# A delta-rule block solve on TensorE taken in two halves of its twenty groups

## What is computed

```python
def delta_attn(x, Wq, Wk, Wv, Wb, Wo, onorm_w):      # b = 5, t = 64, H = 8, DK = DV = 32
    q = l2norm(jax.nn.silu((x @ Wq).reshape(b, t, H, DK)))
    k = l2norm(jax.nn.silu((x @ Wk).reshape(b, t, H, DK)))
    v = jax.nn.silu((x @ Wv).reshape(b, t, H, DV))
    beta = jax.nn.sigmoid(x @ Wb) * 2.0
    def step(S, inps):
        qi, ki, vi, bi = inps
        pred = jnp.einsum('bhkv,bhk->bhv', S, ki)
        S = S + bi[..., None, None] * ki[..., :, None] * (vi - pred)[..., None, :]
        o = jnp.einsum('bhkv,bhk->bhv', S, qi)
        return (S, o)
    _, o = jax.lax.scan(step, S0, (qt, kt, vt, bt))
    return rmsnorm(o, onorm_w).reshape(b, t, H * DV) @ Wo
for l in range(2):
    x = x + delta_attn(rmsnorm(x, norm1_w[l]), ...)
    g, y = jnp.split(rmsnorm(x, norm2_w[l]) @ Wg[l], 2, axis=-1)
    x = x + jax.nn.silu(g) * y @ Wd[l]
```

## Time and profile before

| | |
|---|---|
| median of 3 runs | 403.05 us (402.88 to 404.66) |
| time of the profiled execution | 402.49 us |
| its span, first to last instruction | 400.7 us |
| PE matmul busy | 310.2 us, 77% of the span, 4346 records |
| DVE busy | 201.9 us, 50% |
| ACT busy | 87.7 us, 22% |
| chain that ended last | PE 47%, DVE 31%, DMA 9%, ACT 5%, POOL 4%, issue 3% |
| mean granted PE clock | 0.872 of full speed |

### The profile page before, as it was taken

The page is one execution under the profiler, slowest core; times in us unless marked ns, Lnnn a source line. Parts: engine busy times, 40 slices in busy tenths (PEclk is TensorE's granted clock), DMA queues, the critical chain, the costliest instruction groups (busy, mean ns, idle before and its releaser), DMA issues.

```text
span 400.7 us, 9465 instructions
## 1 busy us (share of the span) xinstructions
PE 310.2 (77%) x4346; PEld 228.6 (57%) x4346; DVE 201.9 (50%) x349; ACT 87.7 (22%) x181; POOL 44.1 (11%) x33
## 2 busy tenths in 40 slices
PE   0999459968972597794776999895676999878965
PEld 0556355757862385472775767573676757555442
DVE  3029977994677443107553222107653232169992
ACT  1132012202210023452111133344121122231120
POOL 0744940200403000000000000000000000000000
PEclk9999958999995578899596799998695699989998
DMA  8999900000000000000000030410000000000001
GB/s 186 334 324 212 362 10 1 2 0 1 2 0 0 0 0 2 0 0 2 3 0 3 2 106 2 151 71 2 3 0 3 2 0 2 1 1 0 2 0 33
DMA packets 2521, 18.26 MB, mean 46 GB/s; under 512 B 441, under 2 KB 761, under 8 KB 1729
## 3 DMA queue, kind: packets, MB, share of 16 engines
q1 hardware_dynamic: 2497, 17.91, 14.6%
HBM read 17.58 MB, written 0.33 MB: 45 GB/s over the span
## 4 chain that ended last, share of the span: by engine, by line
PE 47%; DVE 31%; DMA 9%; ACT 5%; POOL 4%; issue 3%; SPq 1%; DVEq 0%; ACTq 0%; POOLq 0%
PE ps L1221 9%; DMA big<-in_patches 9%; PE ps L1066 5%; PE ps L1217 5%; PE ps L1006 4%; PE ps L1364 3%; POOL xs L262 3%; PE ps L1285 2%; PE ps L1327 2%; DVE big L888 2%; PE ps L1304 2%; PE ps L1016 2%; DVE big L916 2%; DVE qa L569 2%; DVE wt L913 2%
## 5 line engine op out<-in xcount | busy, mean ns | idle before, releaser
L1016 PE MATMUL ps<-big,cwb 120*128 120x384 f32 x120 | 43.6, 523 | 10.3 <-DMA big<-in_patches 10.3
L1016 PEld LDWEIGHTS ps<-big,cwb 120*128 120x128 f32 x120 | 24.4, 207 | 27.1 <-issue 14.3
L1217 PE MATMUL ps<-cst,ones 128*128 128x320 f32 x112 | 37.7, 488 | 0.0
L1066 PE MATMUL ps<-wkvg,pecT 128*128 128x256 f32 x144 | 32.0, 381 | 4.8 <-ACT big L360 4.8
L1221 PE MATMUL ps<-cwb,wl 128*128 128x320 f32 x120 | 33.2, 434 | 0.0
L1066 PEld LDWEIGHTS ps<-wkvg,pecT 128*128 128x128 f32 x144 | 27.0, 190 | 8.6 <-DVE prod L684 3.7
L1217 PEld LDWEIGHTS ps<-cst,ones 128*128 128x128 f32 x112 | 24.0, 219 | 10.6 <-issue 3.9
L1221 PEld LDWEIGHTS ps<-cwb,wl 128*128 128x128 f32 x120 | 22.6, 190 | 10.4 <-issue 0.9
L1285 PE MATMUL ps<-wt,big 32*32 32x32 f32 x1280 | 16.2, 209 | 13.2 <-DVE wt L891 10.5
L262 POOL TENSOR_TENSOR xs<-xs,big 120x640 f32<-120x640 f32 x14 | 23.0, 1645 | 8.2 <-DMA big<-in_patches 7.3
L1285 PEld LDWEIGHTS ps<-wt,big 32*32 32x32 f32 x1280 | 14.5, 121 | 15.3 <-DVE wt L891 11.4
(11 more groups left out here) (224 smaller groups left out, 483.8 us busy)
## 6 DMA issues: line engine op xcount, KB each, us to landing
big<-in_patches SPq DMA_DIRECT2D x6, 900.0 KB, 26.0
wl<-in_layers SPq DMA_DIRECT2D x2, 2176.0 KB, 27.0
wt<-in_tok SPq DMA_DIRECT2D x1, 2304.0 KB, 17.6
wf<-in_ffn SPq DMA_DIRECT2D x1, 2112.0 KB, 26.3
wl<-in_layers SPq DMA_DIRECT2D x2, 1040.0 KB, 23.2
cwb<-in_conv SPq DMA_DIRECT2D x1, 600.0 KB, 5.1
out<-h SPq DMA_DIRECT2D x5, 64.0 KB, 2.0
cst<-in_constants SPq DMA_DIRECT2D x1, 304.0 KB, 39.6
```

The costliest lines, as they stand in the source:

```text
L1016: last = mm(ps[:, i % 4, 0:GRP], cwc[:, k, c * P:(c + 1) * P], xg[:, g, k, :], start=(k == 0), stop=(k == KC - 1))
L1066: last = mm(ps[:, 2 * w + un % 2, t * C:(t + 1) * C], pecT[:, c, i * P:(i + 1) * P], wkvg[:, c, w * C:(w + 1) * C], start=(c == 0), stop=( ...
L1217: mm(ps[:, bank, 0:NT], ones[:, :], cst[:, 0:NT], start=True, stop=True)
```

## The change

All five steps, and the squares and their sums, go in halves `b` = 0 and 1 of ten groups, one bank each. The ACT and DVE instructions of 640 columns become two of 320, and every semaphore of the part is raised once (or, `b2`, twice) per half. PE starts the first half of the first solve when `t` is 1. The output product's first half waits besides until all additions to `bv` are done, since it overwrites the bank that they read. Matmuls, and the data they work on, stay as they are in number and size.

```diff
@@ -166,9 +166,9 @@
 
             return ps[r, b, 0:NT].rearrange("p (g n) -> p g n", n=32)
 
-        def both(x, q):
-
-            return x[32 * q:32 * q + 32, :, :].rearrange("p (a g) n -> p a (g n)", a=2)
+        def half(x, q, b):
+
+            return x[32 * q:32 * q + 32, NB * b:NB * (b + 1), :].rearrange("p g n -> p (g n)")
 
         ident = cst[:, K_ID:K_ID + P]
         blk = cst[:, K_BLK:K_BLK + P]
@@ -198,8 +198,8 @@
         EACH = {
             "lwa": 16, "lwb": 16, "x": 4, "n_sq": 2, "n_ms": 2, "n_rs": 4, "h": 4, "k_mm": 1, "q2_mm": 1, "bt_mm": 1,
             "v_mm": 1, "silu": 10, "ss_mm": 2, "rkq": 4, "kq": 5, "wbx": 1, "ap_mm": 3, "ap": 3, "y_mm": 2 * (LEVELS - 1), "pairs": 8, "y": 2 * (LEVELS - 1),
-            "z_mm": 2 * (LEVELS - 1), "tp": 2 * (LEVELS - 1), "t": 0, "u1_mm": 1, "u1": 1, "u1_two": 1, "r_mm": 1, "b2": 2, "u2_mm": 1, "u2": 1, "u2_two": 1,
-            "o_mm": 1, "osq": 1, "oss": 1, "ors": 2, "on": 1, "o_t": 1, "oT": 3, "wo_mm": 2, "up_mm": FC, "sg": FC,
+            "z_mm": 2 * (LEVELS - 1), "tp": 2 * (LEVELS - 1), "t": 0, "u1_mm": 2, "u1": 2, "u1_two": 2, "r_mm": 2, "b2": 4, "u2_mm": 2, "u2": 2, "u2_two": 2,
+            "o_mm": 2, "osq": 2, "oss": 2, "ors": 2, "on": 1, "o_t": 1, "oT": 3, "wo_mm": 2, "up_mm": FC, "sg": FC,
             "act": FC, "dn_mm": 2,
         }
         S = {n: ctx.enter_context(nc.semaphore("s_" + n)) for n in (*once.split(), *EACH)}
@@ -458,14 +458,17 @@
                             act_.wait_ge(S["z_mm"], EACH["z_mm"] * l + 2 * (lev - 2) + b + 1)
                         nc.scalar.copy(yc[:, NB * b:NB * (b + 1), :], bank32(4 + b, slice(0, P))).then_inc(S["y"], 1)
 
-                act_.wait_ge(S["u1_mm"], EACH["u1_mm"] * l + 1)
-                nc.scalar.copy(both(uc, 0), ps[0:32, 4:6, 0:NT]).then_inc(S["u1"], 1)
-                act_.wait_ge(S["u2_mm"], EACH["u2_mm"] * l + 1)
-                nc.scalar.copy(both(uc, 1), ps[32:64, 4:6, 0:NT]).then_inc(S["u2"], 1)
-                act_.wait_ge(S["o_mm"], EACH["o_mm"] * l + 1)
-                nc.scalar.activation(osq[:, :, :].rearrange("p (a g) n -> p a (g n)", a=2), ps[:, 6:8, 0:NT],
-                                     ACT.Square).then_inc(S["osq"], 1)
-                act_.wait_ge(S["oss"], EACH["oss"] * l + 1)
+                for b in range(2):
+                    act_.wait_ge(S["u1_mm"], EACH["u1_mm"] * l + b + 1)
+                    nc.scalar.copy(half(uc, 0, b), ps[0:32, 4 + b, 0:NT]).then_inc(S["u1"], 1)
+                for b in range(2):
+                    act_.wait_ge(S["u2_mm"], EACH["u2_mm"] * l + b + 1)
+                    nc.scalar.copy(half(uc, 1, b), ps[32:64, 4 + b, 0:NT]).then_inc(S["u2"], 1)
+                for b in range(2):
+                    act_.wait_ge(S["o_mm"], EACH["o_mm"] * l + b + 1)
+                    nc.scalar.activation(osq[:, NB * b:NB * (b + 1), :].rearrange("p g n -> p (g n)"),
+                                         ps[:, 6 + b, 0:NT], ACT.Square).then_inc(S["osq"], 1)
+                act_.wait_ge(S["oss"], EACH["oss"] * l + 2)
                 rsqrt(act_, oss[:, :], oss[:, :], "ors", EPS_RMS, scale=1.0 / DH, k=1, layer=l)
                 norm(l, 1)
                 nc.scalar.preload_act_table_set("silu_and_others")
@@ -916,19 +919,24 @@
                         v.transpose(ttc[:, g, :].rearrange("p g n -> p (g n)"),
                                     tc_[:, g, :].rearrange("p g n -> p (g n)")).then_inc(S["t"], 1)
 
-                dve.wait_ge(S["u1_mm"], EACH["u1_mm"] * l + 1)
-                v.tensor_copy(both(uc, 2), ps[64:96, 4:6, 0:NT]).then_inc(S["u1_two"], 1)
-
-                dve.wait_ge(S["r_mm"], EACH["r_mm"] * l + 1)
-                for a in range(2):
-                    q = 2 * a + 1
-                    v.tensor_tensor(both(bv, q), both(bv, q), ps[32 * q:32 * q + 32, 6:8, 0:NT], ALU.add
-                                    ).then_inc(S["b2"], 1)
-                dve.wait_ge(S["u2_mm"], EACH["u2_mm"] * l + 1)
-                v.tensor_copy(both(uc, 3), ps[96:128, 4:6, 0:NT]).then_inc(S["u2_two"], 1)
-
-                dve.wait_ge(S["osq"], EACH["osq"] * l + 1)
-                v.tensor_reduce(oss[:, :], osq[:, :, :], AX.X, ALU.add).then_inc(S["oss"], 1)
+                for b in range(2):
+                    dve.wait_ge(S["u1_mm"], EACH["u1_mm"] * l + b + 1)
+                    v.tensor_copy(half(uc, 2, b), ps[64:96, 4 + b, 0:NT]).then_inc(S["u1_two"], 1)
+
+                for b in range(2):
+                    dve.wait_ge(S["r_mm"], EACH["r_mm"] * l + b + 1)
+                    for a in range(2):
+                        q = 2 * a + 1
+                        v.tensor_tensor(half(bv, q, b), half(bv, q, b), ps[32 * q:32 * q + 32, 6 + b, 0:NT], ALU.add
+                                        ).then_inc(S["b2"], 1)
+                for b in range(2):
+                    dve.wait_ge(S["u2_mm"], EACH["u2_mm"] * l + b + 1)
+                    v.tensor_copy(half(uc, 3, b), ps[96:128, 4 + b, 0:NT]).then_inc(S["u2_two"], 1)
+
+                for b in range(2):
+                    dve.wait_ge(S["osq"], EACH["osq"] * l + b + 1)
+                    g = slice(NB * b, NB * (b + 1))
+                    v.tensor_reduce(oss[:, g], osq[:, g, :], AX.X, ALU.add).then_inc(S["oss"], 1)
                 dve.wait_ge(S["ors"], EACH["ors"] * l + 2)
                 v.tensor_tensor(osb[:, :, :].rearrange("p (a g) n -> p a g n", a=2),
                                 ps[:, 6:8, 0:NT].rearrange("p a (g n) -> p a g n", n=32),
@@ -1296,37 +1304,43 @@
                         last.then_inc(S["z_mm"], 1)
                     pe.sem_inc(S["y"], -2)
 
-                def solve(rows):
-
-                    for g in range(NG):
+                def solve(rows, b):
+
+                    for g in range(NB * b, NB * (b + 1)):
                         for q in rows:
                             r = slice(32 * q, 32 * q + 32)
-                            last = mm(ps[r, 4 + g // NB, 32 * (g % NB):32 * (g % NB) + 32], ttc[r, g, :],
+                            last = mm(ps[r, 4 + b, 32 * (g % NB):32 * (g % NB) + 32], ttc[r, g, :],
                                       bv[r, g, :], start=True, stop=True)
                     return last
 
 
-                pe.wait_ge(S["t"], 2)
-                solve((0, 2)).then_inc(S["u1_mm"], 1)
+                for b in range(2):
+                    pe.wait_ge(S["t"], b + 1)
+                    solve((0, 2), b).then_inc(S["u1_mm"], 1)
                 pe.sem_inc(S["t"], -2)
-                pe.wait_ge(S["u1"], l + 1)
-                pe.wait_ge(S["u1_two"], l + 1)
-                for g in range(NG):
-                    for a in range(2):
-                        last = mm(ps[64 * a + 32:64 * a + 64, 6 + g // NB, 32 * (g % NB):32 * (g % NB) + 32],
-                                  apm[64 * a:64 * a + 32, g, 32:64], uc[64 * a:64 * a + 32, g, :],
-                                  start=True, stop=True)
-                last.then_inc(S["r_mm"], 1)
-                pe.wait_ge(S["b2"], EACH["b2"] * l + 2)
-                solve((1, 3)).then_inc(S["u2_mm"], 1)
-                pe.wait_ge(S["u2"], l + 1)
-                pe.wait_ge(S["u2_two"], l + 1)
-                for g in range(NG):
-                    for a in range(2):
-                        r = slice(64 * a, 64 * a + 64)
-                        last = mm(ps[r, 6 + g // NB, 32 * (g % NB):32 * (g % NB) + 32], apm[r, g, 64:P], uc[r, g, :],
-                                  start=True, stop=True)
-                last.then_inc(S["o_mm"], 1)
+                for b in range(2):
+                    pe.wait_ge(S["u1"], EACH["u1"] * l + b + 1)
+                    pe.wait_ge(S["u1_two"], EACH["u1_two"] * l + b + 1)
+                    for g in range(NB * b, NB * (b + 1)):
+                        for a in range(2):
+                            last = mm(ps[64 * a + 32:64 * a + 64, 6 + b, 32 * (g % NB):32 * (g % NB) + 32],
+                                      apm[64 * a:64 * a + 32, g, 32:64], uc[64 * a:64 * a + 32, g, :],
+                                      start=True, stop=True)
+                    last.then_inc(S["r_mm"], 1)
+                for b in range(2):
+                    pe.wait_ge(S["b2"], EACH["b2"] * l + 2 * b + 2)
+                    solve((1, 3), b).then_inc(S["u2_mm"], 1)
+                for b in range(2):
+                    pe.wait_ge(S["u2"], EACH["u2"] * l + b + 1)
+                    pe.wait_ge(S["u2_two"], EACH["u2_two"] * l + b + 1)
+                    if b == 0:
+                        pe.wait_ge(S["b2"], EACH["b2"] * (l + 1))
+                    for g in range(NB * b, NB * (b + 1)):
+                        for a in range(2):
+                            r = slice(64 * a, 64 * a + 64)
+                            last = mm(ps[r, 6 + b, 32 * (g % NB):32 * (g % NB) + 32], apm[r, g, 64:P], uc[r, g, :],
+                                      start=True, stop=True)
+                    last.then_inc(S["o_mm"], 1)
```

## The result

| | before | after |
|---|---|---|
| median of 4 runs | 403.86 us (402.88 to 405.31) | 392.51 us (391.95 to 394.63) |
| profiled execution, span | 402.49, 400.7 us | 392.98, 391.2 us |
| PE, DVE, ACT busy | 310.2, 201.9, 87.7 us | 309.1, 204.0, 88.7 us |
| mean granted clock | 0.872 | 0.878 |

The ratio is 0.9732, 95% interval 0.9687 to 0.9777: 9.0 to 12.6 us less. The forecast was 394.0 (389.0 to 398.0). The medians lie 11.4 us apart, the two profiled executions 9.5; what follows is read from those two.

What follows compares the result with a forecast made beforehand. Bound by a strict PE-DVE relay in each layer's solve chain, one engine working at a time; 2 x 4.9 − 0.6 − 0.2 = 9.0 us off 402.49 gives 393.5, plus 0.56 for the median: 394.0 us, range 389.0 to 398.0.

Steps and rivals of the forecast that it cites:

- The relay becomes an overlap: Last transposed inverse to output transposes: halves let PE work while DVE copies and adds; waiting goes, all work stays.
- Layer 1, 4.9 us: Layer 1's chain: output product ends at 310.54 instead of 315.48 us, 4.9 us earlier, with the clock falling at 301.4.
- Layer 0, 4.9 us: Layer 0's chain: output product ends at 218.79 instead of 223.65 us, 4.9 us earlier, with the clock falling at 212.8.
- The signs: Trace marks: second transpose to output product's end 9.2 to 9.9 us, PE idle under 1 us, four additions of 0.49.
- Tail halves worth nothing, keep_clock releases the transposes: Behind the output product: halved squares and sums gain nothing, since the transposes begin only when keep_clock ends.
- keep_clock, 0.3 us a layer charged: Behind the output product: 0.3 us a layer charged because the clock's return need not move with the work.
- 5.3 to 5.7 for a low keep_clock: Behind the output product: estimated keep_clock time in us if the clock stays low throughout, against 4.24 and 2.85 wholly high.
- Rival, the clock stays high: Through one or both layers' chains: nearly gapless PE holds 2.4 GHz, 4.3 us more a layer, 390 or 385.5; chance 0.10.
- The split's fixed cost: DVE's halves: 2 x 0.49 against 0.83 us, 0.15 more each; five more instructions a layer, not on the chain.
- The number: Whole kernel: 9.0 us saved, profiled execution 402.49 to 393.5 us, median forecast 394.0.

Runs made afterwards that it cites:

- k4: Changed kernel with squares and their sums in one piece again instead of halves; 392.48 us in a single run.
- k9: Changed kernel plus three wide filler matmuls a layer, one ahead of the first solve and one behind each half of the second; 392.31 us, single run.
- k10: Changed kernel plus 256 records of small matmuls between level loop and first solve, written out one by one; 407.1 us, single run.
- k8: Changed kernel plus sixteen small matmuls near PE's start, read by nobody; median 398.77 us, ratio to before 0.9871.
- k11: Changed kernel plus 256 records of small matmuls between level loop and first solve, as a hardware loop of sixteen passes; 414.4 us, single run.

## Why the prediction was right, by its steps

- **The relay becomes an overlap**: right. Copies left the chain, PE's only waits for DVE that end on the chain behind the first solve are 0.22 and 0.43 us, and DVE's halves took 0.48 to 0.50 us, ACT's 0.41 to 0.42, as taken from the earlier trace rows. No disturbance between banks.
- **Layer 1, 4.9 us**: measured 4.8. **Layer 0, 4.9 us**: measured 3.7. The step that was short is the residual product's second half, "so it runs 211.06 to 211.79": the forecast took gapless PE work to cost only its own time. PE stood for 0.88 us with no semaphore to wait for, the second additions came at 213.06 to 214.08 instead of 212.10 to 213.10, and the output product ended 1.0 us late. The clock also fell 3.5 us behind the start of the first solve where 4.15 was assumed. Layer 1 paused for 0.72 us too, but its clock fell 4.4 us behind that start where 1.7 was assumed, which paid for it: that its 4.9 came true to 0.1 is luck.
- **The signs**: the forecast wanted 9.2 to 9.9 us from the second transpose to the end of the output product and PE idle there under 1 us. It was 10.4 and 10.1 us, with 1.2 and 1.3 us idle. These two signs failed, by the pause and by the waits of 0.22 and 0.43 us for the additions, where the layer 1 of the forecast had none. The others held: the residual product right behind the first solve, four additions of about 0.49 us, transposes released by keep_clock, a low clock in the output product.
- **Tail halves worth nothing, keep_clock releases the transposes**: right (k4).
- **keep_clock, 0.3 us a layer charged**: −0.1 and +0.3. In the variants with five matmuls it was 4.1 to 5.6, mostly near 5, so the charge was small; with the clock held it was 2.9, as bounded. The forecast's 5.3 to 5.7 for a low keep_clock should have read 5.7 to 5.8 by its own rows (twice 2.85, and twice ten eighths of 2.32).
- **Rival, the clock stays high**: did not happen here; in one layer of k9, with fillers, it did, and the output product, estimated at 2.8 us for a high clock, took 2.45.
- **The split's fixed cost**: five more DVE instructions a layer; DVE's busy time rose by 2.1 us in all (ten times 0.15 would be 1.5), and the copies' share of it is off the chain.
- **The number**: the profiled gain of 9.5 is 7.8 of the chains and what lies between and 1.7 of the clock at the end. Without that luck the forecast of 9.0 would have been 1.2 too large; it was saved by a term that I did not have. The medians, 11.4 us apart, moved further than the forecast; part of this is before's median, 403.86 here against the 403.05 from which the forecast set out, and the rest is not placed, since only one execution of each was traced.

## What to carry to other kernels

A relay between two engines over two independent banks is worth splitting when the trace shows each waiting for the whole of the other; lay the halves out in time, since the gains of the parts did not add up here. When PE's waits are gone, look at its program itself: fp32 matmuls of 32 columns, written out, can run faster than their instructions arrive, and the trace then says "issue" in the middle of a product, at a place that moves with the length of the code ahead. Before you call added work free, look in the trace where it stands. Judge such a change by its own stage, because the clock elsewhere moves the total by more than its last microsecond.

## Not expected of the hardware

- PE stopped for 0.1 to 2.3 us at borders of 128 matmul records of written-out code, at some of them only; in k10 it went on 3.45 and 3.46 us apart. Code added some 190 us earlier moved the stop by its length (k8).
- A hardware loop of 16 records a pass took 0.44 us a pass, almost three times what the same matmuls took written out between two stops (k11: 256 records in 7.05 us; k10: 149 in 1.45).
- Three filler matmuls were followed by a held clock in one layer and a fallen one in the other, in the same run (k9).
